# Moving the operand sums of a seven-product scheme from GpSimd to VectorE, and a maximum's spread from GpSimd to TensorE, in a two-layer graph network

## The reference

```python
def sage(h, W_self, W_neigh, b):
    agg = segment_sum(h[src], dst)           # A^T h, A = counts of edges
    return h @ W_self + (agg / max(deg, 1)) @ W_neigh + b
h   = relu(sage(x, Ws0, Wn0, b0))
out = layernorm(x + sage(h, Ws1, Wn1, b1))
```

## Time and profile before

| | us |
|---|---|
| median of 3 runs | 703.18 |
| lowest, highest | 700.7, 704.2 |
| the profiled execution | 703.99 |
| its span | 702.2 |

### The profile page before, as it was taken

The page is one execution under the profiler, slowest core; times in us unless marked ns, Lnnn a source line. Parts: engine busy times, 40 slices in busy tenths (PEclk is TensorE's granted clock), DMA queues, the critical chain, the costliest instruction groups (busy, mean ns, idle before and its releaser), DMA issues.

```text
span 702.2 us, 11075 instructions
## 1 busy us (share of the span) xinstructions
PE 632.6 (90%) x3284; PEld 324.9 (46%) x3284; DVE 504.2 (72%) x1143; ACT 254.5 (36%) x460; POOL 220.9 (31%) x273
## 2 busy tenths in 40 slices
PE   3888989998999999999997659999999878799995
PEld 3734545544666666555543224444444333344442
DVE  7896477769777874499899746552360989987764
ACT  5663634443343434012444424442001343333321
POOL 3002136532333334000453362200221878622100
PEclk9999999999999999999999879999999998999998
DMA  8623000000000000314220000000583354311111
GB/s 322 228 108 132 1 1 0 0 1 1 1 0 1 0 0 0 122 61 133 76 89 32 0 0 1 1 0 1 194 321 145 116 177 162 141 61 60 61 60 54
DMA packets 16142, 50.33 MB, mean 72 GB/s; under 512 B 2616, under 2 KB 2776, under 8 KB 16096
## 3 DMA queue, kind: packets, MB, share of 16 engines
q1 hardware_dynamic: 16096, 49.77, 19.6%
HBM read 40.45 MB, written 9.31 MB: 71 GB/s over the span
## 4 chain that ended last, share of the span: by engine, by line
PE 54%; DVE 24%; issue 9%; DMA 6%; ACT 3%; POOL 2%; SPq 1%; POOLq 0%; DVEq 0%; ACTq 0%
PE ps L810 19%; PE ps L713 14%; PE ps L686 10%; DVE xz L1362 5%; PE ps L610 4%; PE ps L844 4%; DMA ws<-in_L_gnn_W_neigh 3%; DVE wn L1370 3%; DMA scratch<-in_x 2%; DVE scratch L1353 2%; DVE ws L1362 2%; DVE scratch L1346 2%; DVE wn L306 1%; DVE hmx L1339 1%; DVE scratch L1458 1%
## 5 line engine op out<-in xcount | busy, mean ns | idle before, releaser
L810 PE MATMUL ps<-xz,wn 128*128 128x512 f16 x600 | 135.6, 386 | 14.9 <-DVE wn L1370 9.0
L686 PE MATMUL ps<-wn,xz 128*128 128x512 f16 x480 | 116.6, 383 | 2.8 <-DVE wn L306 1.4
L480 POOL TENSOR_TENSOR A<-A,scratch 128x120 int32 x160 | 72.5, 453 | 140.3 <-ACT scratch L872 110.4
L713 PE MATMUL ps<-xz,ws 128*128 128x420 f16 (+1 forms) x576 | 116.2, 339 | 0.0
L1152 DVE TENSOR_SCALAR lohot<-iota_lo,table 125x128 f16<-125x128 f16 x320 | 86.9, 272 | 25.3 <-PE ps L610 24.7
L1154 DVE TENSOR_SCALAR scratch<-iota_q,table 125x240 f16<-125x240 f16 x320 | 103.8, 324 | 0.3 <-issue 0.2
L872 ACT ACTIVATE scratch<-ps 128x240 uint16<-128x240 f32 x160 | 58.9, 370 | 121.5 <-PE ps L610 102.0
L810 PEld LDWEIGHTS ps<-xz,wn 128*128 128x128 f16 x600 | 58.9, 99 | 89.9 <-issue 14.5
L752 PE MATMUL ps<-A,zh 128*128 128x420 f16 (+1 forms) x480 | 85.6, 340 | 2.7 <-DVE scratch L1353 2.4
L844 PE MATMUL ps<-wn,A 128*128 128x512 f16 x200 | 77.0, 385 | 7.1 <-DVE scratch L1458 7.1
L844 PE MATMUL ps<-ws,A 128*128 128x512 f16 x200 | 76.9, 384 | 0.0
(11 more groups left out here) (171 smaller groups left out, 747.5 us busy)
## 6 DMA issues: line engine op xcount, KB each, us to landing
ws<-in_L_gnn_W_neigh SPq DMA_DIRECT2D x16, 512.0 KB, 4.5
wn<-in_L_gnn_W_self SPq DMA_DIRECT2D x16, 512.0 KB, 5.2
zh<-in_x SPq DMA_DIRECT2D x9, 512.0 KB, 7.9
scratch<-in_x SPq DMA_DIRECT2D x9, 512.0 KB, 6.6
ws<-in_L_gnn_W_neigh SPq DMA_DIRECT2D x4, 1024.0 KB, 16.5
ws<-in_L_gnn_W_self SPq DMA_DIRECT2D x4, 1024.0 KB, 8.7
partial<-scratch SPq DMA_DIRECT2D x8, 512.0 KB, 3.7
wn<-partial SPq DMA_DIRECT2D x4, 512.0 KB, 7.0
```

Source lines behind the costliest of these rows:

```text
L480: pool.tensor_tensor(a, a, stage32[0:TP, r], ALU.add).then_inc(counts_added, 1)
L686: ins = pe.matmul(ps[0:TP, 2 * r + half, :], lhs(a, k, t), w[:, k, b, half * HD:(half + 1) * HD], start=(k == 0 and a == 0 and b == 0), st ...
L713: ins = pe.matmul(ps[:, b, 0:CH[n]], ws[:, k, a, bass.ds(f * P, P)], xT[h][:, k, CO[n]:CO[n] + CH[n]], start=(k == 0 and a == 0 and h == 0 ...
L810: ins = pe.matmul(ps[:, b, :], slot[:, k, a, :], Tm[m][:, k, w, :], start=(m in (1, 2, 5) and k == 0 and a == 0 and w == 0), stop=(k == HK ...
```

## The change

- `t_sum4` and `s_sum` move from GpSimd to VectorE. In the A stage the four sums of a piece stand in every fourth unit from (2,0) on. `STEP7` spreads the high and low parts of a piece over four units (two, two, three, none), where `PARTS` had three units, and starts them one block of features earlier. In the product loops `s_sum(e + 7)` stands right ahead of `item_lows(e + 7)`.
- The weight magnitudes are no longer a maximum on VectorE, but a sum of magnitudes by row on ScalarE (`weight_sums`, `ACT.Abs` with an accumulator), two instructions for each piece. SP's loads wait for these.
- h's maximum is spread by TensorE: VectorE multiplies the identity by it, TensorE multiplies by ones behind product 0, and VectorE reduces the bank. `spread("h")` is gone, and `s_z1` is made ahead of the product loop instead of in step e == 1.
- In the tile stage `residual` 0 to 2 stand ahead of `spread` for ws1 and the others behind it without anything between. VectorE's t_sum4 and t_lows stand behind `y_tile` 3 to 6 (t_lows: 4 to 7 before). SP's raw loads stand at other steps.

```diff
-        ORDER = ["b0", "ws0", "wn1", "h", "ws1"]
+        ORDER = ["b0", "ws0", "wn1", "ws1"]
...
             if 2 <= u < HK + 2:
-                eng.wait_ge(max_done, HK * phase + u - 1)
+                eng.wait_ge(max_done, 2 * (HK * phase + u - 1))
...
-                for u in {0: (2,), 1: (3,), 2: (4, 5), 4: (6,), 5: (7,)}.get(f, ()):
+                for u in {0: (2, 3), 1: (4, 5), 3: (6,), 5: (7,)}.get(f, ()):
                     load_raw(sp, 0, u)
...
             for n in range(2):
                 load_x(n)
+            for u in range(2, HK):
+                load_raw(sp, 1, u)
...
-                for u in {0: (2,), 1: (3,), 2: (4, 5), 4: (6,), 5: (7,)}.get(n, ()):
+                for u in {0: (4, 5), 3: (6,), 4: (7,)}.get(n, ()):
                     load_raw(sp, 1, u)
...  (GpSimd: t_sum4 and s_sum gone)
-            for n in range(4):
+            for n in range(3):
                 residual(n)
-            spread(4)
-            pool.wait_ge(item_low, NP7)
-            for k in range(HK):
-                residual(4 + k)
-                t_sum4(1, k)
-            for n in range(4 + HK, JT):
+            spread(3)
+            for n in range(3, JT):
                 residual(n)
...  (TensorE)
             for e in range(NP7):
                 product(0, e)
+                if e == 0:
+                    pe.wait_ge(diag_ready, 3)
+                    pe.matmul(ps[:, 6, 0:P], ones[:], hdiag, start=True, stop=True).then_inc(diag_spread, 1)
...  (ScalarE)
+            def weight_sums(phase, k, dump):
+                raw_landed(act, phase, k)
+                m = MC[("wn1", "ws1")[phase]] + 2 * k
+                for q in range(2):
+                    act.activation(dump, wraw[phase][k % 2][:, q, :], ACT.Abs,
+                                   accum_out=mx[:, m + q:m + q + 1]).then_inc(max_done, 1)
...
+                    for k in {(0, 0): (0,), (0, 1): (1,), (1, 0): (2,), (1, 1): (3,)}.get((f, n), ()):
+                        weight_sums(0, k, unread)
...
+            for k in range(HK):
+                weight_sums(1, k, unread)
             act.wait_ge(scale_ready, 6)
...  (VectorE, A stage)
+                    u = 3 * f + n - 6
+                    if 1 <= u <= 4 * HK:
+                        t_lows(0, (u - 1) // 4, STEP7[(u - 1) % 4])
+                    if u % 4 == 0 and 0 <= u < 4 * HK:
+                        for i in range(4):
+                            t_sum4(0, u // 4, i)
             item_lows(0, 0)
             hmax(KT - 1, 2)
+            dve.wait_ge(h_tail_zero, 1)
+            s_sum(0, 2)
+            item_lows(0, 1)
+            s_sum(0, 3)
             dve.wait_ge(hmax_done, 3 * KT)
-            dve.tensor_reduce(c("maxh"), hmx[:], AX.X, ALU.max).then_inc(maxes_ready, 1)
-            for e in range(1, ITEMS):
+            link(dve.tensor_reduce(c("maxh"), hmx[:], AX.X, ALU.max))
+            dve.tensor_scalar(hdiag, ident[:], c("maxh"), None, ALU.mult).then_inc(diag_ready, 1)
+            item_lows(0, 2)
+            s_sum(0, 4)
+            item_lows(0, 3)
+            s_sum(0, 5)
+            dve.wait_ge(diag_spread, 3)
+            link(dve.tensor_reduce(c("allh"), ps[:, 6, 0:P], AX.X, ALU.max))
+            pow2("hs", c("allh"))
+            link(dve.tensor_scalar(c("s_z1"), c("r_hs"), 2.0 ** -9, None, ALU.mult))
+            signal(scale_ready)
+            for e in range(4, ITEMS):
                 item_lows(0, e)
...  (both product loops)
                 if e + ITEMS < NP7:
+                    s_sum(0, e + ITEMS)
                     item_lows(0, e + ITEMS)
...  (tile stage)
-                for k in {0: (0, 1), 1: (2,), 2: (3,)}.get(n, ()):
-                    wmax(1, k)
+                if n == 1:
+                    dve.wait_ge(max_done, 4 * HK)
+                    tensor_max("ws1", KT, MC["ws1"])
...
-                if 4 <= n < 4 + HK:
-                    t_lows(1, n - 4, range(ITEMS))
+                if 3 <= n < 3 + HK:
+                    for i in range(4):
+                        t_sum4(1, n - 3, i)
+                    t_lows(1, n - 3, range(ITEMS))
                 if n == JT - 2:
+                    dve.wait_ge(t_low, 2 * ITEMS * HK)
+                    for e in range(ITEMS):
+                        s_sum(1, e)
```

More of the change, by code:

```diff
@@ L423, in _ @@
                 load_x(n)
+            for u in range(2, HK):
+                load_raw(sp, 1, u)
+            for n in range(2):
                 tile_slices(n)
@@ L560, in _ @@
             ins.then_inc(h_tail_zero, 1)
-            pool.wait_ge(h_tail_zero, 1)
-            pool.wait_ge(h32_ready, 3 * KT)
-            for i in range(4):
-                s_sum(i)
-            spread(3)
-            for i in range(4, 4 * IT):
-                s_sum(i)
             pool.wait_ge(b1_in, 16)
@@ L1002, in item @@
                 act.activation(ring[g % SLOTS][:, :, 0, :], operand(p, m), ACT.Copy).then_inc(item_high, 1)
+            def weight_sums(phase, k, dump):
[4 more added lines that the diff above has]
+                                   accum_out=mx[:, m + q:m + q + 1]).then_inc(max_done, 1)
+                    act.wait_ge(max_done, 2 * (HK * phase + k) + q + 1)
             for f in range(KT):
-                for n, some in enumerate(((0, 1), (2, 3), (4, 5, 6))):
+                for n in range(3):
                     unit(f, n)
-                    if f == 3 and n == 0:
+                    q = 3 * f + n - 6
+                    for k in {(0, 0): (0,), (0, 1): (1,), (1, 0): (2,), (1, 1): (3,)}.get((f, n), ()):
+                        weight_sums(0, k, unread)
+                    if q == 0:
                         act.wait_ge(scale_ready, 4)
-                    if 3 <= f < 3 + HK:
-                        for i in some:
-                            t_item(0, f - 3, i)
+                    for i in STEP7[q % 4] if 0 <= q < 4 * HK else ():
+                        t_item(0, q // 4, i)
                     if f == KT - 1 and n == 0:
@@ L1434, in _ @@
                 if e == 1:
-                    dve.wait_ge(max_spread, ORDER.index("h") + 1)
-                    pow2("hs", c("allh"))
-                    link(dve.tensor_scalar(c("s_z1"), c("r_hs"), 2.0 ** -9, None, ALU.mult))
-                    signal(scale_ready)
                     mul("ca1", "p_h", "p_wn1", 2.0 ** -16)
@@ L1500, in _ @@
                 if e + ITEMS < NP7:
+                    s_sum(1, e + ITEMS)
                     item_lows(1, e + ITEMS)
```

83 lines of the change are left out of this document (36 added, 47 removed).

## The result

The changed kernel takes 697.99 us (median, 695.27 to 701.54) against 703.78 for the kernel before on the same chips: a ratio of 0.992 (95% interval 0.990 to 0.994). It is faster, by 5.8 us where 13.9 had been forecast. Its profiled execution took 701.54 us (span 699.9), 3.5 above its median, so stages are also compared with a second profile of the same kernel (`e1`, span 696.1).

What follows compares the result with a forecast made beforehand. TensorE was taken as the long engine up to the second products, where VectorE sets the pace. Terms -2.7 - 3.3 - 9.7 - 0.7 - 7.7 + 10.2 = -13.9 from 703.99 give 690.1, forecast 690.0 us (0.981), range 682 to 700.

Steps and rivals of the forecast that it cites:

- A stage, -2.7: A stage: VectorE just keeps pace without slow low parts, so TensorE's 2.7 us of idle time goes.
- Gap ahead of product 0, -3.3: Between A stage and first products: TensorE's gap falls from 5.7 to 2.4 us.
- First products, -9.7: First products: 95.5 us in place of 105.2, with pairs still bounded by TensorE at 18.13 us.
- stall of 2.2 after product 3: First products: product 3 could start at 11.1 us but waits for kept(5) until some 13.3, a stall of 2.2.
- Rival 1: First products: VectorE bounds them too, pairs of 19.5 us, 695 to 702 us in all; chance 0.22.
- rival 3: Placed at product 3 of the first products: sum, high part, low part, kept result lock into one chain; 712 us; chance 0.11.
- Tile stage, -0.7: Tile stage: one stall at ws1's spread, then VectorE at 9.0 us a tile for four tiles; 95.0 us long.
- All those overlaps go, since GpSimd has no sums any more: VectorE's low parts no longer lengthened by GpSimd's sums; 0.69 us gained a piece in the second products, two a pair.
- Start of the second products, -7.7: Second products up to step 6: no gap ahead of product 0, and step 6 ends at 22.2 us, before at 26.5.
- Three pairs, +10.2: Second products, three pairs to step 27: 3.4 us more each on VectorE, 22.7 in place of 19.3.
- two prices: Tile stage, ws1's spread on GpSimd: 9.47 us of issue taken; with about 6 us, stall 3.5 us shorter and forecast 687.

Runs made afterwards that it cites:

- e6: Changed kernel with the A stage's weight sums back on GpSimd, in the changed order: 700.18 us, ratio 0.996.
- e2: Changed kernel with GpSimd's residual adding the bias in one of 1024 columns only, the other columns' bias left out: 687.45 us, ratio 0.975.
- e7: Changed kernel with the second products' sums back on GpSimd and ws1's maximum spread by TensorE behind tile 2: 678.13 us, ratio 0.964.
- e9: Changed kernel with the residual moved from GpSimd to the head of y_tile on VectorE, ws1's spread staying on GpSimd: 687.93 us, ratio 0.978.
- e10: Changed kernel with each sum of the second products made one step earlier on VectorE, no instruction added or removed: 682.43 us, ratio 0.972.

## Why the prediction fell short

Its steps in order, with the profiled execution for the change (703.99 to 701.54, spans 702.2 to 699.9).

- **A stage, -2.7.** Measured 88.2 to 84.7, -3.5. The size was nearly right and half the reason was not: `e6` has the slow low parts back and no idle time. That leaves the removed magnitudes, the four units and the earlier start, which no run separates.
- **Gap ahead of product 0, -3.3.** Measured -3.2.
- **First products, -9.7.** Measured -11.4. The sum charged a stall of 2.2 after product 3 and a slow stretch of 1.7. The changed kernel has the slow stretch in product 0 (4.44 us for 12 matmuls) and a stall of only 0.33. In `e2`, `e6` and `e7` product 0 runs at the high clock (2.75 us) and the stall is 1.84, and the stage is 93.65 us all the same. The two stand for one wait, and one of them was counted too many. Rival 1 didn't occur (pairs 18.13), and rival 3 neither at its place.
- **Tile stage, -0.7.** Measured +8.1 (95.8 to 103.9; +5.4 in `e1`). This is the step that failed. Its first half held: residual(2) done at 31.2 where 28.5 was said, tile 5 at 48.5 where 46 to 50 was said, the stall 5.16 within 3 to 7. The failure is the next sentence, VectorE at 9.0 us a tile for four tiles, and it rests on "All those overlaps go, since GpSimd has no sums any more". GpSimd still had ten residuals of 2.4 us, which also read two SBUF tiles. VectorE's own work is 8.7, but the meetings make the four tiles 9.5, 10.8, 10.8 and 12.9, 9.1 us more, against TensorE's 8.63. With 8.7 a tile the last tile would end 92.1 us into the stage, which is the good end of the 92.4 to 96.1 of the sum; the 9.1 of the meetings and the 2.7 of the slow clock behind the last stall make it 103.9. `e2` takes the residuals' work away and has 88.8, `e9` moves it and has 86.4.
- **Start of the second products, -7.7.** Measured -6.9 (additions of step 6 at 619.01 and 602.66, from the ends of the tile stages at 589.8 and 580.35).
- **Three pairs, +10.2.** Measured +14.1. The mechanism was right and the term 3.9 us too small: 3.4 a pair gave 22.7, and the pair in which the clock stayed high was 23.0. The other two were 24.6 and 24.4, since the sum had no term for TensorE's clock behind the waits that the longer pairs give it. The price of a step's round trip was right, 1.38 against 1.43 (612.30 to 613.73).

The two misses are 8.8 and 3.9 us, the start of the second products adds 0.8, and the first stages gave back 2.4. That makes -2.8 of the forecast -13.9, and the profiled spans differ by -2.3. The medians differ by -5.8, since this profiled execution took 3.5 us more than its median; `e1`, 1.7 us below its own median, has the tile stage without the 2.7 of slow clock. The same two steps are off in both profiles. Both misses have a common part, the slow clock behind new stalls: 2.7 us behind the last stall of the tile stage (none in `e1`) and some 1.6 in two of the three pairs. The 2.6 behind the stall of tile 5 cost nothing, since TensorE waits for VectorE again ahead of tiles 8 and 9 (2.01, 4.11).

The prediction priced an overlap by a row in which GpSimd's instruction was a sum of 1.27 us: 0.69. Beside a residual of 2.4 us the price was 2.1. The Trainium skill (SBUF — State Buffer, Who interferes with whom) says that a VectorE instruction of two SBUF inputs contends with a GpSimd instruction that reads SBUF, and it calls the contention for the shared ports an exclusive lock. The rows with residuals agree: at 540.37 and 562.12 a residual had some 2.3 us left (540.14 and 2.52, 562.01 and 2.39), and VectorE's instruction was 2.1 longer. The prediction used this rule for the removed sums alone and not for what stayed.

For the spread the prediction had two prices. The Trainium skill (GPSIMD Engine Reference, 2.1 Instruction dispatch) has about 6 us for the first call of a freshly loaded program; the changed kernel had 5.80 in this place, and the prediction took the 9.47 of the earlier trace rows. That error went the other way and hid part of the miss.

Rival 3's chain exists, though not where it was put. In the second products each summed step waits 0.76 us for ScalarE, and `e10` breaks it by order alone.

What stays open: why the clock fell behind the stalls of 5.16, 4.11 and 2.79 and once not behind 2.79 (650.49). In `e1` it fell behind 2.02 and not behind 2.31. The 2.7 us between the two profiles of the tile stage are the last tile's share of this.
